# Output weights folded into the key-value sums, queries normalised and turned, one key-query product, and a plain fp32 output projection

## The chip, the cores and the metric

The kernel runs on one core of a Trainium2 chip. Its engines work side by side, each through its own queue of instructions in program order, and wait for one another through semaphores: PE (TensorE, matrix products into PSUM), DVE (VectorE), ACT (ScalarE), POOL (GpSimd) and SP (SyncE, which issues DMA transfers here). The metric is the time of one launch in device microseconds (us), the median of several runs.

## The reference

Input x has 4 batches of 2,048 tokens with 256 features. In fp32:

```
x = x + attn_a(layernorm(x))    # linear attention, 16 heads of 16
x = x + ffn(layernorm(x))       # square(relu(x @ Ws1)) @ Ws2, and routed experts
x = x + attn_b(layernorm(x))    # softmax attention, changes the first 16 tokens of a batch
x = x + ffn(layernorm(x))

# attn_a:
q = elu(x @ Wq + bq) + 1;  k = elu(x @ Wk + bk) + 1;  v = x @ Wv + bv
kv  = einsum('bkhd,bkhm->bhdm', k, v)
out = einsum('bqhd,bhdm->bqhm', q, kv)
normalizer = max(einsum('bqhd,bkhd->bqh', q, k), 1e-6)
out = (out / normalizer[..., None]).reshape(B, S, D) @ Wo + bo
```

The experts' weights are truncated, so they count only if a flag says that some weight reached 1; with these inputs the flag is 0 and the branches on it (`routed > 0`) are not taken.

## The kernel before, in words

The 8,192 tokens are 16 groups (`NG`) of 512, each of 4 tiles (`T`) of 128 tokens; D = 256 is C = 2 blocks of 128. x stays in SBUF (`x_all`) for the whole launch.

**Pass 1** goes over the 16 groups: layer norm 1, transposes of the normalised tokens, the key product by tokens (24 matmuls of 256 columns, operands split into a high and a low part), the query product by features (12 matmuls of 512 columns), exponentials, and G = kᵀx (`g_product`, L1334 and L1339: 8 of 512 and 8 of 256 columns). After each batch the sum G is turned and multiplied with Wv (`kv_product`), masked by head, and stored in `kv_all` with a column per head for the key sums. The queries stay in SBUF, features on partitions (`q_all`).

**Pass 2** goes over steps i = 0 to 17. Step i does the attention output of group i, the first FFN of group r = i − 1 and the second FFN of group v = i − 2. A piece of the small attention attn_b, on the 16 first tokens of each batch, is called in slots between them (`chain(i, slot)`); steps 3 and 4 have no such piece. On PE a step is, in order: T2, transposes of x of group r (L1473); o, queries by key-value sums with the norm in extra columns (L1483); the second FFN's down product (`down`, L1462, into PA); the first FFN's up product (f1, L1504); OT, transposes of the normalised o (L1510); r2, 1/variance turned (L1517); W, the output projection, 24 matmuls of split operands (L1538, L1539, L1544); f3 (L1548); and the first FFN's down product (L1462, into PB).

DVE's queue in a step: the norm out of PSUM (L1035), its reciprocal (L1039), 1/variance (`reciprocal_variances`, L1014, semaphore `rsq`), o times the norm (L1045), the second FFN's sum for two tiles (`scaled_sum`, L1023), o_lo, the low part of the turned o (L1064), h2s (L1071), x plus W (w_add, L1079) with its statistics (bn2, L1003), x plus the FFN (L1087) with its statistics (bn3, L1003). ACT scales the second FFN's other two tiles (`scale_tiles`, L736) into y3. POOL makes the variances (`four_variances`, L491 to L498, five operations for each of the two norms), adds a row to x (`add_row`, L452, 128x1024: `bo` in pass 1, `ob` in pass 2) and adds y3 to x (L550, 128x512). The order of each queue is the order of these calls in the text; no planner moves anything.

Of the kernel before, what the change touches and what calls it, by code (L numbers as in the profile page):

```python
# [13 lines left out]
P = 128  # L14
# [4 lines left out]
T = 4  # L19
# [25 lines left out]
def hybrid_kernel(nc, x_in, Wq, bq, Wk, bk, Wv, bv, Wo, bo, qw, qb, kw, vw, vb, ow, ob,  # L45
# [18 lines left out]
    with ExitStack() as ctx:  # L64
# [11 lines left out]
        q_all = sb("q_all", [P, NG * C, GT])  # L76
        kv_all = sb("kv_all", [P, B * C, KVW])
# [3 lines left out]
        wo_hi, wo_lo = sb("wo_hi", [P, C, D], F32R), sb("wo_lo", [P, C, D], F32R)  # L81
# [17 lines left out]
        norm_sb = sb("norm_sb", [P, T * C, HC])  # L99
        norm_inv = sb("norm_inv", [P, T * C, HC])  # L100
# [31 lines left out]
        o_tok = part(T * D).rearrange("p (k n) -> p k n", k=T * C)  # L132
        x2t = part(C * GT).rearrange("p (c n) -> p c n", c=C)
        h2, h3 = part(GT), part(GT)
        y3 = part(T * D // 2).rearrange("p (t d) -> p t d", d=D)
        token_of = part(B * P)
        squares = o_tok.rearrange("p k n -> p (k n)").rearrange("p (c n) -> p c n", c=C)

        with ExitStack() as pass1_memory:
# [10 lines left out]
            wq_hi, wq_lo = sb1("wq_hi", [P, C, D]), sb1("wq_lo", [P, C, D])  # L150
            wk_hi, wk_lo = sb1("wk_hi", [P, C, D]), sb1("wk_lo", [P, C, D])
            xt_hi, xt_lo = sb1("xt_hi", [P, C, GT]), sb1("xt_lo", [P, C, GT])
            part = parts(sb1("wvo", [P, 9 * D], F32))
            g_sb = part(C * D).rearrange("p (c n) -> p c n", c=C)
            wv = part(C * D).rearrange("p (c n) -> p c n", c=C)
            bo_rows = part(D)
            wo_raw = part(C * D).rearrange("p (c n) -> p c n", c=C)
            wv_last, bv_rows = part(D), part(D)

        part = parts(sb("ffn_weights", [P, 5376 - GT])[:, :])  # L160
        w1c = part(C * F).rearrange("p (c f) -> p c f", c=C)
# [25 lines left out]
        raw4 = [b_weights[:, 1, i, :].rearrange("p (c n) -> p c n", c=C) for i in range(4)]  # L187
        folded_all = b_weights[:, 0, :, :].rearrange("p i n -> p (i n)")
# [18 lines left out]
        used_q = [carve(q_all[:, b * G * C:(b * G + 1) * C, :].rearrange("p k n -> p (k n)")) for b in range(B)]  # L207
# [4 lines left out]
        after_raw = carve(b_weights[:, 1, :, :].rearrange("p i n -> p (i n)"))  # L212
# [8 lines left out]
        later_q = [carve(q_all[:, (b * G + 1) * C:(b * G + 2) * C, :].rearrange("p k n -> p (k n)")) for b in range(B)]  # L221
# [7 lines left out]
        def one_batch_columns(wide):  # L229
# [1484 lines left out]
```

## Time and profile before

| | |
|---|---|
| median of 3 runs | 434.23 us (433.89 to 434.29) |
| span of the profiled execution | 432.7 us |
| PE busy | 416.6 us (96%) |
| DVE busy | 316.3 us (73%) |
| ACT busy | 217.6 us (50%) |
| POOL busy | 217.1 us (50%) |
| granted clock of PE, mean | 0.997 |

The profile has a record of one execution. The span runs from its first to its last instruction; the median of the runs is 1.5 us longer than the span. Busy shares are averages over stages. The views used below are the busy times, windows over stretches of the span, timelines (one line for each instruction or run of like ones, with start and duration), and the instructions of one source line. "L1462" is line 1462 of the kernel before; lines of the changed kernel are told as such.

### The profile page before, as it was taken

The page shows a single profiled execution, that of the slowest core. Times are in us where ns is not written, and L with a number is a line of the kernel's source. Part 1 is how long each engine was busy: PE and PEld are TensorE (multiplying, and loading weights), DVE is VectorE, ACT ScalarE, POOL GpSimd, SP SyncE. Part 2 cuts the span into 40 slices and gives each one's busy share as a digit, 9 for nine tenths or more (in the row PEclk, how much of TensorE's full clock was granted, in tenths as well). Part 3 has the DMA queues.
Part 4 walks back from the last instruction along what each step waited for, and adds up shares of the span by engine and source line. Part 5 has one row for each costly group of instructions (what it writes and reads, how often), then busy time and mean ns, then how long its engine had stood idle before and what let it go on. Part 6 is the DMA issues. An engine that isn't in the chain of part 4 may idle for free.

```text
span 432.7 us, 7753 instructions
## 1 busy us (share of the span) xinstructions
PE 416.6 (96%) x2570; PEld 345.7 (80%) x2570; DVE 316.3 (73%) x707; ACT 217.6 (50%) x383; POOL 217.1 (50%) x317
## 2 busy tenths in 40 slices
PE   8998999999999999899999999999999999999993
PEld 5787889988987988889788886787887787787862
DVE  6769977676668766647878887877778767787864
ACT  3766777778777775326434342343244324334341
POOL 3675776776677764031345336534516416514532
PEclk9999999999999999999999999999999999999998
DMA  8701221111100000300110111011001010011103
GB/s 264 245 7 46 57 88 54 51 49 48 48 0 0 2 2 1 101 0 6 51 52 20 36 51 52 2 51 50 21 31 35 18 52 27 26 51 50 50 4 106
DMA packets 22793, 20.59 MB, mean 48 GB/s; under 512 B 3271, under 2 KB 22733, under 8 KB 22733
## 3 DMA queue, kind: packets, MB, share of 16 engines
q1 hardware_dynamic: 22172, 19.32, 14.1%
q8 instruction: 30, 0.49, 0.5%
q10 hardware_dynamic: 560, 0.52, 0.4%
q14 instruction: 31, 0.25, 0.2%
HBM read 11.32 MB, written 8.45 MB: 46 GB/s over the span
## 4 chain that ended last, share of the span: by engine, by line
PE 68%; DVE 8%; ACT 7%; POOL 7%; issue 5%; SPq 2%; DMA 1%; DVEq 1%; POOLq 0%; ACTq 0%
PE PB L1462 7%; PE PT L1504 6%; PE PA L1462 6%; PE PB L1483 6%; PE PA L1538 4%; PE PA L1544 4%; PE PA L1539 3%; PE PT L1548 3%; PE PA L1473 3%; ACT scratch L568 3%; PE PB L1510 3%; POOL ln_rstd L441 2%; PE PG L1334 2%; POOL ln_rstd L439 2%; DVE ln_bn L800 2%
## 5 line engine op out<-in xcount | busy, mean ns | idle before, releaser
L491 POOL TENSOR_TENSOR ln_a<-ln_bn 128x4 f32<-128x4 f32 x32 | 6.5, 203 | 136.1 <-DVE ln_bn L1003 136.1
L463 POOL TENSOR_TENSOR xn_pair<-scratch,xn_pair 128x1024 fp32r<-128x1024 f32 x16 | 38.4, 2402 | 18.9 <-ACT xn_pair L579 18.9
L883 DVE SCALAR_TENSOR_TENSOR scratch<-scratch,PB 128x512 f32<-128x512 f32 x32 | 20.9, 684 | 36.4 <-ACT scratch L615 36.3
L1003 DVE BATCH_NORM_STATS2 ln_bn<-x_all 128x6 f32<-128x256 f32 x128 | 44.9, 412 | 0.9
L568 ACT ACTIVATE scratch<-x_all,ln_shift,ln_rstd 128x255 f32 (+1 forms) x60 | 31.2, 593 | 22.6 <-POOL ln_shift L445 22.6
L452 POOL TENSOR_TENSOR x_all<-x_all,wvo 128x1024 f32 (+1 forms) x16 | 38.6, 2410 | 0.1
L452 POOL TENSOR_TENSOR x_all<-x_all,ob_rows 128x1024 f32<-128x1024 f32 x16 | 37.7, 2356 | 0.0
L1307 PE MATMUL PB<-wk_hi,xt_hi 128*128 128x256 f32 x128 | 36.9, 288 | 0.6 <-DVE xt_lo L828 0.4
L1309 PE MATMUL PB<-wk_hi,xt_lo 128*128 128x256 f32 x128 | 36.2, 283 | 0.0
L1308 PE MATMUL PB<-wk_lo,xt_hi 128*128 128x256 f32 x128 | 36.2, 283 | 0.0
L736 ACT ACTIVATE scratch<-PA,ln_rsq 128x256 f32<-128x256 f32 x30 | 12.6, 471 | 45.4 <-PE PA L1462 40.2
L1334 PE MATMUL PG<-xn_pair,o_hi 128*128 128x512 f32 x128 | 33.7, 405 | 1.1 <-ACT o_hi L623 1.1
L1079 DVE TENSOR_TENSOR x_all<-PA,x_all 128x1024 f32<-128x1024 f32 x16 | 19.6, 1225 | 19.5 <-PE PA L1544 19.5
L758 ACT ACTIVATE o_hi<-PB 128x512 fp32r<-128x512 f32 x32 | 17.4, 594 | 32.5 <-PE PB L1510 32.5
L1538 PE MATMUL PA<-wo_hi,o_hi 128*128 128x256 f32 x128 | 33.4, 293 | 0.0
L774 ACT ACTIVATE scratch<-PT,w1ob 128x512 f32<-128x512 f32 x16 | 11.0, 688 | 42.1 <-PE PT L1548 42.1
L1539 PE MATMUL PA<-wo_lo,o_hi 128*128 128x256 f32 x128 | 31.9, 282 | 0.0
L1462 PE MATMUL PB<-ws,h2s 128*128 128x256 f32 x128 | 31.0, 385 | 0.0
L1504 PE MATMUL PT<-scratch,ffn_weights 128*128 128x512 f32 x64 | 30.9, 605 | 0.0
L1462 PE MATMUL PA<-ws,scratch 128*128 128x256 f32 x128 | 30.2, 379 | 0.0
L1064 DVE TENSOR_TENSOR o_lo<-PB,o_hi 128x512 fp32r<-128x512 f32 x32 | 20.6, 686 | 12.0 <-ACT o_hi L758 11.8
L1462 PEld LDWEIGHTS PB<-ws,h2s 128*128 128x128 f32 x128 | 23.6, 190 | 6.6 <-issue 3.9
(247 smaller groups left out, 1139.0 us busy)
## 6 DMA issues: line engine op xcount, KB each, us to landing
x_all<-n_L_attn_a_inputs_q_dram SPq DMA_DIRECT2D x15, 512.0 KB, 3.5
out_dram<-x_all SPq DMA_DIRECT2D x15, 512.0 KB, 3.1
out_dram<-x_all SPq DMA_DIRECT2D x2, 256.0 KB, 2.2
x_all<-n_L_attn_a_inputs_q_dram ACTq DMA_DIRECT2D x2, 128.0 KB, 3.0
x_all<-n_L_attn_a_inputs_q_dram SPq DMA_DIRECT2D x2, 128.0 KB, 2.7
setup<-in_L_attn_a_Wk_dram SPq DMA_DIRECT2D x1, 256.0 KB, 4.6
setup<-in_L_attn_a_Wq_dram ACTq DMA_DIRECT2D x1, 256.0 KB, 5.0
wvo<-in_L_attn_a_Wv_dram SPq DMA_DIRECT2D x1, 256.0 KB, 6.7
```

The costliest lines, as they stand in the source:

```text
L452: nc.gpsimd.tensor_tensor(x_group(n), x_group(n), rows_[:, :].rearrange("p (o d) -> p o d", o=1).to_broadcast([P, T, D]), ALU.add).then_in ...
L463: nc.gpsimd.tensor_tensor(xn_pair[:, :, 1, :], xn[g % 2], xn_pair[:, :, 0, :].bitcast(F32), ALU.subtract).then_inc(x_lo, 1)
L568: nc.scalar.activation(dst[:, t:t + 1, 0:width], x_tile(n, t)[:, :, 0:width], ACT.Identity, scale=ln_rstd[:, slot, t:t + 1], bias=ln_shift ...
L1003: nc.vector.bn_stats(ln_bn[:, slot, t:t + 1, :], x_tile(n, t)).then_inc(bn, 1)
L1307: mm(dst, hi, wk_hi[:, c, :], start=(c == 0), stop=False)
L1308: mm(dst, hi, wk_lo[:, c, :], start=False, stop=False)
L1309: last = mm(dst, lo, wk_hi[:, c, :], start=False, stop=(c == C - 1))
L1334: mm(PG[:, c, :], k_hi[:, t, c * P:(c + 1) * P], xn_pair[:, t, :, :].rearrange("p h d -> p (h d)"), start=(g == 0 and t == 0), stop=False, ...
L1462: last = mm(four(pair)[:, t, :], h[:, t * P:(t + 1) * P], ws2[:, :], start=True, stop=True)
L1504: last = mm(PT[:, 0, :], w1c[:, c, :], x2t[:, c, :], start=(c == 0), stop=(c == C - 1))
L1538: mm(four(PA)[:, t, :], hi, wo_hi[:, c, :], start=(c == 0), stop=False)
L1539: mm(four(PA)[:, t, :], hi, wo_lo[:, c, :], start=False, stop=False)
```

## The change

1. **Folded weights.** After each batch, `m_product` multiplies the masked key-value sums with Wo and keeps `m_sum[b]` (256x256); the key sums are kept as one row of 256 for all partitions (`ksum`). In pass 2 the o product is gone.
2. **Queries by token.** Key and query weights stand side by side, so that one product by tokens gives both (24 matmuls of 512 columns; L1322 to L1324 go). `q_all` has tokens on partitions. POOL multiplies queries by key sums (`q_product`), DVE sums by head, bounds, inverts, and multiplies the queries in place (`query`), and PE turns the normalised queries. `query(i + 1)` is called in step i.
3. **Plain fp32 projection.** W is 8 matmuls of fp32 operands; the split of Wo and o_lo are gone.
4. **Smaller moves.** All four tiles of y3 are scaled by ACT and added by POOL (128x1024), save for the last two groups (`by_dve`); the variances of both norms are five POOL operations after bn3 (`variances`); x plus the FFN is added in two halves; the loops over batches in pass 1 are unrolled, its work goes by halves of a group, and `fold_ffn` moves ahead of the last G product.

```diff
+            def q_product(j):  # POOL
+                n, b = lagged(j // B, j % B, 0)[1:]
+                pool.wait_ge(ksum_done, b + 1)
+                pool.wait_ge(q_done, 2 * (n + 1))
...
+                    pool.wait_ge(q_norm, 3 * (j - 1) + 1)
+                nc.gpsimd.tensor_tensor(prod.rearrange("p (t d) -> p t d", t=T), q_all[:, n * T:(n + 1) * T, :],
+                                        ksum[:, b:b + 1, :].to_broadcast([P, T, D]), ALU.mult).then_inc(q_prod, 1)
...
+            def query(j):  # DVE
+                n = lagged(j // B, j % B, 0)[1]
+                by_head = q_all[:, n * T:(n + 1) * T, :].rearrange("p t (h e) -> p (t h) e", e=HD)
+                dve.wait_ge(q_prod, j + 1)
+                nc.vector.reduce_sum(norm_sb[:, :], prod.rearrange("p (k e) -> p k e", e=HD), AX).then_inc(q_norm, 1)
+                dve.wait_ge(q_norm, 3 * j + 1)
+                nc.vector.tensor_scalar(norm_sb[:, :], norm_sb[:, :], NORM_EPS, None, ALU.max).then_inc(q_norm, 1)
+                dve.wait_ge(q_norm, 3 * j + 2)
+                nc.vector.reciprocal(norm_inv[:, :], norm_sb[:, :]).then_inc(q_norm, 1)
+                dve.wait_ge(q_norm, 3 * j + 3)
+                nc.vector.tensor_tensor(by_head, by_head, norm_inv[:, :].unsqueeze(2).to_broadcast([P, T * H, HD]),
+                                        ALU.mult).then_inc(q_ready, 1)
...
+            def m_product(b):  # PE
+                pe.wait_ge(kv_masked, C * (b + 1))
+                pe.wait_ge(ksum_done, b + 1)
+                for c in range(C):
+                    last = mm(PG[:, 1, c * D:(c + 1) * D], kvt[:, c, :], wo_raw[:, c, :], start=True, stop=True)
+                last.then_inc(m_mm, 1)
...
-                    for tiles in ((0, 2), (1, 3)):
+                    pe.wait_ge(m_done, b + 1)
+                    for t in range(T):
                         for c in range(C):
-                            pe.wait_ge(o_hi_done, C * i + c + 1)
-                            for t in tiles:
-                                hi = o_hi[:, c, t * P:(t + 1) * P]
-                                mm(four(PA)[:, t, :], hi, wo_hi[:, c, :], start=(c == 0), stop=False)
-                                mm(four(PA)[:, t, :], hi, wo_lo[:, c, :], start=False, stop=False)
...
+                            pe.wait_ge(ot_copied, C * i + c + 1)
+                            last = mm(four(PA)[:, t, :], o_t[:, c, t * P:(t + 1) * P], m_sum[b][:, c, :],
+                                      start=(c == 0), stop=(c == C - 1))
...
             def scale_tiles(i, v):  # ACT
-                for t in range(2, T):
+                for t in range(by_dve(v), T):
...
             def step(g, b):  # DVE
-                if runs(i):
-                    for c in range(C):
-                        dve.wait_ge(o_hi_done, C * i + c + 1)
-                        nc.vector.tensor_tensor(o_lo[:, c, :], PB[:, c, :], o_hi[:, c, :].bitcast(F32),
-                                                ALU.subtract).then_inc(o_lo_done, 1)
+                if i + 1 < NG:
+                    query(i + 1)
                 if runs(r):
                     dve.wait_ge(f1_sq, r + 1)
```

How the queues move shows best in the instructions themselves. **DVE in step 3 of pass 2.** Before (PT, PA, PB: PSUM; scratch: working rows in SBUF):

```order
L1035 TENSOR_SCALAR norm_sb<-PT 128x16 [waits o_mm]
L1035 TENSOR_SCALAR norm_sb<-PB 128x24 x2
L1039 RECIPROCAL norm_inv<-norm_sb 128x64 [waits o_norm]
L1014 RECIPROCAL ln_rsq<-ln_a 128x8 [waits var3,f4_scaled,r2_mm,var2]
L1045 TENSOR_TENSOR scratch<-PT,norm_inv 128x256 [waits ot_mm,o_norm]
L1045 TENSOR_TENSOR scratch<-PB,norm_inv 128x384 x2
L1023 SCALAR_TENSOR_TENSOR x_all<-PA,ln_rsq,x_all 128x256 [waits c_xs,rsq,f4_mm]
L1023 SCALAR_TENSOR_TENSOR x_all<-PA,ln_rsq,x_all 128x256
L1064 TENSOR_TENSOR o_lo<-PB,o_hi 128x512 [waits w_mm,o_hi_done] x2
L1071 TENSOR_TENSOR h2s<-scratch,PT 128x512 [waits f2_mm,r2_mm,f1_sq]
L1079 TENSOR_TENSOR x_all<-PA,x_all 128x1024 [waits bo_added,w_mm]
```

The changed kernel, from 1/variance (L1056) on:

```order
L1056 RECIPROCAL ln_rsq<-ln_a 128x8 [waits f4_scaled,r2_mm,var]
L943 TENSOR_REDUCE norm_sb<-scratch 128x64 [waits q_prod,rsq,f4_mm]
L945 TENSOR_SCALAR norm_sb<-norm_sb 128x64 [waits q_norm]
L947 RECIPROCAL norm_inv<-norm_sb 128x64 [waits q_norm]
L949 TENSOR_TENSOR q_all<-q_all,norm_inv 128x1024 [waits q_norm]
L1088 TENSOR_TENSOR scratch<-scratch,PT 128x512 [waits r2_mm,f1_sq]
L1096 TENSOR_TENSOR x_all<-PA,x_all 128x1024 [waits bo_added,w_mm]
L1046 BN_STATS ln_bn<-x_all 128x6 [waits var,w_added]
L1046 BN_STATS ln_bn<-x_all 128x6 x3
L1105 TENSOR_TENSOR x_all<-PB,x_all 128x512 [waits f2_mm,ob_added]
L1105 TENSOR_TENSOR x_all<-PB,x_all 128x512 [waits f2_mm]
L1046 BN_STATS ln_bn<-x_all 128x6 [waits var,f2_added]
```

The four instructions of the norm that read PSUM ahead of 1/variance and behind it are gone, with the scaled sum and o_lo. Four instructions of query for the next group, all on SBUF, stand between 1/variance and h2s; w_add and what follows come behind them.

**POOL in the same step.** Before:

```order
L491 TENSOR_TENSOR ln_a<-ln_bn 128x4 [waits bn2,rsq]
L492 TENSOR_TENSOR ln_d<-ln_bn 128x4
L494 TENSOR_SCALAR ln_a<-ln_a 128x4 [waits var2]
L496 TENSOR_TENSOR ln_d<-ln_d 128x4 [waits var2]
L498 TENSOR_TENSOR ln_a<-ln_a,ln_d 128x4 [waits var2]
L491 TENSOR_TENSOR ln_a<-ln_bn 128x4 [waits bn3]
L492 TENSOR_TENSOR ln_d<-ln_bn 128x4
L494 TENSOR_SCALAR ln_a<-ln_a 128x4 [waits var3]
L496 TENSOR_TENSOR ln_d<-ln_d 128x4 [waits var3]
L498 TENSOR_TENSOR ln_a<-ln_a,ln_d 128x4 [waits var3]
L452 TENSOR_TENSOR x_all<-x_all,ob_rows 128x1024 [waits t2_mm]
L550 TENSOR_TENSOR x_all<-x_all,scratch 128x512 [waits f4_scaled]
```

The changed kernel:

```order
L489 TENSOR_TENSOR scratch<-q_all,ksum 128x1024 [waits q_norm,q_done,ksum_done]
L521 TENSOR_TENSOR ln_a<-ln_bn 128x8 [waits bn3,bn2,rsq]
L522 TENSOR_TENSOR ln_d<-ln_bn 128x8
L524 TENSOR_SCALAR ln_a<-ln_a 128x8 [waits var]
L526 TENSOR_TENSOR ln_d<-ln_d 128x8 [waits var]
L528 TENSOR_TENSOR ln_a<-ln_a,ln_d 128x8 [waits var]
L466 TENSOR_TENSOR x_all<-x_all,ob_rows 128x1024 [waits t2_mm]
L582 TENSOR_TENSOR x_all<-x_all,scratch 128x1024 [waits c_xs,f4_scaled]
```

The product q_product stands at the head of the step, the variances of both norms are one run of five, and the sum of y3 covers 1,024 elements where it covered 512.

**DVE at the end of pass 1**, group 15 of the changed kernel (L867: key features, L870: query features, L876: the low part of the keys, for G):

```order
L861 TENSOR_TENSOR xt_lo<-PT,xt_hi 128x2x256 [waits t1_hi]
L867 SCALAR_TENSOR_TENSOR scratch<-scratch,PA 128x512 [waits k_hi_done,kq_exp]
L870 SCALAR_TENSOR_TENSOR q_all<-scratch,PA 128x512
L876 TENSOR_TENSOR o_lo<-scratch,o_hi 128x512 [waits k_hi_done]
L943 TENSOR_REDUCE norm_sb<-scratch 128x64 [waits q_prod]
L945 TENSOR_SCALAR norm_sb<-norm_sb 128x64 [waits q_norm]
L947 RECIPROCAL norm_inv<-norm_sb 128x64 [waits q_norm]
L949 TENSOR_TENSOR q_all<-q_all,norm_inv 128x1024 [waits q_norm]
L867 SCALAR_TENSOR_TENSOR scratch<-scratch,PB 128x512 [waits k_hi_done,kq_exp]
L870 SCALAR_TENSOR_TENSOR q_all<-scratch,PB 128x512
L876 TENSOR_TENSOR o_lo<-scratch,o_hi 128x512 [waits k_hi_done]
```

The query of group 0 stands between the two halves of the last group's features, and waits there for POOL's first q_product.

## Rows read from the trace of the kernel before

**Rows 1.** The page's first part (busy time, share, instructions) and its chain of waits.

```profile
span 432.7 us, 7753 instructions
...
PE 416.6 (96%) x2570; PEld 345.7 (80%) x2570; DVE 316.3 (73%) x707; ACT 217.6 (50%) x383; POOL 217.1 (50%) x317
...
PE 68%; DVE 8%; ACT 7%; POOL 7%; issue 5%; SPq 2%; DMA 1%; DVEq 1%; POOLq 0%; ACTq 0%
```

**Rows 2.** Windows by stage; columns: us, busy of each engine, granted clock, DMA share, GB/s.

```profile
0.00:170.34 170.34, 163.79 (x1006) 141.13 (x1007) 122.31 (x264) 121.45 (x196) 114.99 (x112) 1.00 0.20 61
170.34:197.60 27.26, 25.82 (x197) 23.45 (x196) 16.41 (x38) 9.79 (x21) 3.81 (x7) 1.00 0.16 41
197.60:411.46 213.86, 213.76 (x1312) 171.95 (x1311) 165.71 (x380) 80.22 (x154) 91.90 (x182) 1.00 0.11 37
```

**Rows 3.** Windows: one plain step, one with side chain.

```profile
228.73:242.18 13.45, 13.45 (x83) 11.13 (x82) 10.30 (x24) 5.45 (x10) 5.43 (x12) 1.00 0.13 41
256.09:272.66 16.57, 16.57 (x94) 12.21 (x93) 12.86 (x31) 5.45 (x10) 8.51 (x14) 1.00 0.10 34
```

**Rows 4.** Timeline of the plain step, PE: start, duration, engine, line, operation.

```profile
228.73 1.04 PE L1473 MATMUL PA<-ident,x_all 128*128 128x128 f32 x8
...
229.60 0.63 PE L1483 MATMUL PT<-kv_all,q_all 128*128 128x136 f32 x4
...
231.70 1.89 PE L1462 MATMUL PA<-ws,scratch 128*128 128x256 f32 x8
...
233.43 1.88 PE L1504 MATMUL PT<-scratch,ffn_weights 128*128 128x512 f32 x4
...
236.59 0.36 PE L1538 MATMUL PA<-wo_hi,o_hi 128*128 128x256 f32 x1
...
239.60 1.02 PE L1548 MATMUL PT<-h2s,ffn_weights 128*128 128x512 f32 x2
...
242.18 0.49 PE L1473 MATMUL PA<-ident,x_all 128*128 128x128 f32 x3
```

**Rows 5.** Timeline of the same step, DVE, ACT and POOL.

```profile
230.19 1.41 DVE L1003 BATCH_NORM_STATS2 ln_bn<-x_all 128x6 f32<-128x256 f32 x4
...
232.81 2.35 POOL L452 TENSOR_TENSOR x_all<-x_all,ob_rows 128x1024 f32<-128x1024 f32 x1
233.06 0.20 DVE L1014 RECIPROCAL ln_rsq<-ln_a 128x8 f32<-128x8 f32 x1 [0.21 <-POOL ln_a L498]
...
233.63 0.84 ACT L736 ACTIVATE scratch<-PA,ln_rsq 128x256 f32<-128x256 f32 x2 [3.12 <-PE PA L1462]
...
238.12 0.69 DVE L1071 TENSOR_TENSOR h2s<-scratch,PT 128x512 f32<-128x512 f32 x1 [0.35 <-ACT scratch L766]
...
239.80 1.22 DVE L1079 TENSOR_TENSOR x_all<-PA,x_all 128x1024 f32<-128x1024 f32 x1 [0.99 <-PE PA L1544]
```

**Rows 6.** Timeline, DVE and POOL, at 34 us and at 407 us.

```profile
33.77 2.41 POOL L452 TENSOR_TENSOR x_all<-x_all,wvo 128x1024 f32<-128x1024 f32 x1
...
34.24 2.49 DVE L844 TENSOR_TENSOR wvo<-wvo 128x512 f32<-128x512 f32 x1
...
406.76 1.27 POOL L550 TENSOR_TENSOR x_all<-x_all,scratch 128x512 f32<-128x512 f32 x1
...
406.85 1.32 DVE L1235 TENSOR_SCALAR b_weights<-q_all,ffn_weights 64x256 f32<-64x256 f32 x1
```

**Rows 7.** Instructions of one line: count, duration in ns (least, median, most), first and last start.

```profile
L1039 DVE RECIPROCAL norm_inv<-norm_sb x16: 553/553/554, 175.9 to 403.9; 128x64 f32<-128x64 f32 x16
...
L890 DVE TENSOR_TENSOR o_lo<-scratch,o_hi x16: 1183/1226/2611, 19.8 to 169.9; 128x1024 fp32r<-128x1024 f32 x16
```

**Rows 8.** Timeline, POOL and DVE, at 62.6 us.

```profile
62.54 1.06 POOL L441 TENSOR_TENSOR ln_rstd<-ln_rstd,minus_half 128x4 f32<-128x4 f32 x1
62.62 1.22 DVE L890 TENSOR_TENSOR o_lo<-scratch,o_hi 128x1024 fp32r<-128x1024 f32 x1
```

**Rows 9.** Timeline, PE: the G product of two groups of pass 1.

```profile
143.25 2.11 PE L1334 MATMUL PG<-xn_pair,o_hi 128*128 128x512 f32 x8
...
152.55 2.12 PE L1334 MATMUL PG<-xn_pair,o_hi 128*128 128x512 f32 x8
```

More of the change, by code:

```diff
@@ L318, in runs @@
         def runs(j):
[L320 to L325 removed]
+            return 0 <= j < NG
         @block.sync
@@ L537, in step @@
                 v, nv, _ = lagged(g, b, 2)
[L538 to L542 removed]
+                if i + 1 < NG:
+                    q_product(i + 1)
+                if runs(r) or runs(v):
+                    ge(pool, rsq, i - 1)
+                    variances(i, r, v)
                 if runs(r):
@@ new lines, in _ @@
+            act.wait_ge(consts, 4)
+            x_high(0, 0)
+            normalise(1)
+            for n in range(NG):
+                g, b = n % G, n // G
+                exponentials(n, 0)
+                x_high(n, 1)
+                k_high(n, 0)
+                if n + 1 < NG:
+                    xt_high(n + 1, 0)
+                if g == 0 and b > 0:
+                    transposed_g(b - 1)
+                if n + 2 < NG:
+                    normalise(n + 2)
+                if g == 1 and b > 0:
+                    m_copy(b - 1)
+                exponentials(n, 1)
+                if n + 1 < NG:
+                    xt_high(n + 1, 1)
+                k_high(n, 1)
+                if n + 1 < NG:
+                    x_high(n + 1, 0)
@@ new lines, in _ @@
+            for n in range(NG):
+                g, b = n % G, n // G
+                k_features(n, 0)
+                if g == 0 and b > 0:
+                    copy_g(b - 1)
+                q_features(n, 0)
+                k_low(n, 0)
+                if n + 1 < NG:
+                    xt_low(n + 1, 0)
+                if n + 3 < NG:
+                    stats(n + 3)
+                if n == 1:
+                    dve.wait_ge(w2_loaded, 16 * 8)
+                    take_last_row(wv, wv_last, bv_rows, wv_row, 0.0)
+                if n == NG - 1:
+                    query(0)
+                k_features(n, 1)
+                q_features(n, 1)
+                if g == 0 and b > 0:
+                    batch_kv(b - 1)
+                k_low(n, 1)
+                if n + 1 < NG:
+                    xt_low(n + 1, 1)
@@ new lines, in _ @@
+            for n in range(NG):
+                g, b = n % G, n // G
+                if n == 0:
+                    first_kq()
+                else:
+                    kq(n, 0)
+                    g_product(n - 1, 1)
+                if n + 1 < NG:
+                    t1(n + 1)
+                if g == 0 and b > 0:
+                    g_transposes(b - 1)
+                if g == 1 and b > 0:
+                    m_product(b - 1)
+                if n > 0:
+                    kq(n, 1)
+                if g == 0 and b > 0:
+                    kv_product(b - 1)
+                elif n == 0:
+                    pe.wait_ge(flag_ready, 1)
+                g_product(n, 0)
```

727 lines of the change are left out of this document (322 added, 405 removed).

## The prediction

> **What bounds the kernel now.** I read the page first. TensorE (PE) is busy for 416.6 of 432.7 us and holds 68% of the chain of waits [rows 1]; so far this is a PE-bound kernel. Then the windows by stage: pass 1 takes 170.3 us, the crossing into pass 2 (up to the end of W for group 1) 27.3, the fourteen steps up to the end of W for group 15 take 213.9, and 21.2 remain for the tail. In the fourteen steps PE is busy for 213.76 of 213.86 us at a granted clock of 1.00 (its upper level, 2.4 GHz), VectorE (DVE) for 165.7 and GpSimd (POOL) for 91.9 [rows 2]. A step without side chain takes 13.45 us, all of it PE's, with 10.3 of DVE and 5.4 of POOL; one with a chain takes 16.6, with 12.9 and 8.5 [rows 3]. Matmul records overlap, so I price PE from start to start. Last I read one plain step, first on PE [rows 4], then on the other engines [rows 5].
>
> The span of the profiled execution is 432.7 us, 1.5 below the median of 434.23; I make the sum on the span and add the 1.5 at the end.
>
> **PE's part.** In the plain step the product of queries and key-value sums (L1483) takes 231.70 − 229.60 = 2.10 us. The split W takes 239.60 − 236.59 = 3.01. Both go. The new W is 8 plain fp32 matmuls of 256 columns, two records each. The same form stands at L1462, where 8 records take 233.43 − 231.70 = 1.73, 0.216 each [rows 4]; 16 records take 3.46. Turning the normalised queries replaces turning the outputs, 8 transposes for 8. PE's step becomes 13.45 − 2.10 − 3.01 + 3.46 = 11.8. If PE still bounded, 14 steps and the crossing would give some 25 us back.
>
> **DVE's and POOL's part.** DVE loses the norm and the multiplication from PSUM, the o_lo of the split and the two-tile scaled sum. It gains query(): a reduction of 1,024 elements (I take 1.2, from L1079 at 1.22 for as many elements [rows 5]; half to twice that is possible), a max over 64 (0.2, the size of L1014's 0.20), a reciprocal (0.55, the same form at L1039 [rows 7]) and q times norm_inv over 1,024 (1.2, from L890's 1.23 [rows 7]). By busy time DVE stays near 10.9 us and does not bound. What matters is where it stands: in DVE's queue query() of the next group comes right behind rsq (L1056) and ahead of h2s and w_add, and it meets POOL's two long adds.
>
> What the rows show of that meeting: a DVE addition of 512 elements with both inputs in SBUF lasts 2.49 us while POOL's add_row (L452, 2.41) runs and ends 0.55 after it, although 512 elements need 0.69 at L1071 with one input in PSUM. A TENSOR_SCALAR over 256 lasts 1.32 where POOL's L550 runs, and ends 0.14 after it [rows 6]. DVE instructions that read PSUM are not held: L1079 and the like keep 1.22. A reciprocal keeps 0.553 in all 16 steps [rows 7]. The Trainium skill ("SBUF — State Buffer", section Who interferes with whom) says that DVE's second SBUF input and its two-port modes share a port pair with GpSimd, that whoever issues first holds it for the instruction, and that the other is fully blocked. The trace agrees on the two long additions; it disagrees at POOL's pow, 1.06 us long, beside which L890 with two SBUF inputs keeps 1.22 [rows 8]. By the rule that row would be 0.98 us longer; in pass 2 no pow stands, so my sum is the same either way.
>
> Now a plain step, counted from rsq = R (233.06 in rows 5). add_row runs from R − 0.25 to R + 2.1, as now. The reduction ends at R + 1.4. The max has one input from SBUF, like the held TENSOR_SCALAR: it waits for add_row, ends at R + 2.25, and the reciprocal at R + 2.85. By then POOL is in the sum of y3 (L582, now all four tiles, 2.35 like L452): its last scaled tile comes from ACT at R + 2.15 (L736 begins at R + 0.57; two take 0.84, four 1.58), so it runs to R + 4.5. The multiplication, with two SBUF inputs, waits for that and ends at R + 5.7; h2s, 0.7, at R + 6.4. W could have ended earlier: it needs the scaled tiles out of PSUM (R + 2.15), then 3.46 and 0.2 to DVE [rows 5], R + 5.8. So w_add begins at R + 6.4, held by DVE's queue. Behind it to the next rsq: w_add 1.22, statistics 1.40, f2's addition in two halves 2 × 0.69, statistics 1.40, and POOL's five small operations with their hops 1.46 (statistics end at 231.60, rsq at 233.06). These are 6.9. **The step takes 13.3 us, against 13.45 now**: PE's 1.65 is given to the multiplication's wait, and PE idles 1.5 per step.
>
> Side chains: DVE was busy for 165.71 − 14 × 10.30 = 21.5 us with them in the fourteen steps [rows 2, 3]. Under a full PE that was partly hidden; now DVE's queue is the loop, and it counts in full. In a chained step it stands between rsq and query, or between query and w_add; then the next q_product, which waits only for the reduction, can begin before the multiplication gets its turn, another 2.4 of POOL. From 0 to all of the 12 chained steps can pay it; I take half, 6 × 2.4 = 14.4. Fourteen steps: 14 × 13.3 + 21.5 + 14.4 = 222.1, that is **+8.2** (bounds −6.2 and +22.6).
>
> **Pass 1.** 24 products of 256 columns and 12 of 512 become 24 of 512: the same columns, and the same period of 9.3 [rows 9]. Each batch adds 2 records for ksum and 4 for Wo folded in (m_product), 6 × 0.216 = 1.3 us. If PE waits there anyway for the copies of G, none of it shows; if not, four batches make 5.2. I take 1.5, nearer to nothing, since these records stand between copies. In the first groups the exponentials start only when keys and queries are both there: 1 more. **+2.5** (0 to +6).
>
> **Crossing.** query(0) now stands ahead of the last key features on DVE, and G, the sums of the last batch and everything of pass 2 wait for those. At the least that is query unheld, 1.2 + 0.2 + 0.55 + 1.2 = 3.15, less the 0.55 of today's reciprocal on the same path: +2.6. At the most one addition of bo on POOL holds it for 2.4 more: +5.0. I take the middle, **+3.8**. At nothing I cost the variances in five POOL operations in place of ten (1.46 from statistics to rsq stays, and that is counted above), the gather on SP, which now waits for the turned queries and not for the o product (the chain reads it later), and the unrolled loops of pass 1 (instructions are fetched ahead; if not, pass 1 grows and the range's upper end has it). Tail: 0; the last two groups keep part or all of their sum on DVE.
>
> **Sum**: 432.7 + 8.2 + 2.5 + 3.8 = 447.2, plus the 1.5: **449 us**.
>
> **Rivals.**
> A, faster: the max is not held. Then the reciprocal ends at R + 2.15, before y3's last tile has reached POOL, the multiplication takes the port first and ends at R + 3.35, h2s at R + 4.05; w_add waits for W, R + 5.8, and the step is 12.7. 14 × 12.7 + 21.5 = 199.3, −14.6; with +2.5, +2.6 and the 1.5 that is 424.7, **425 us**. It is decided by whether the reciprocal ends before R + 2.2. For it: the max has 64 elements, the held one 256. Against it: rows 6, and that DVE would have to win in every step. If chains hide under PE too, PE's full 25 us bring 409.
> B, no change: each step is held as I say, but no q_product slips in: 432.7 − 6.2 + 2.5 + 3.8 + 1.5, **434 us**.
> C, slower still: q_product slips in at every chained step, 463, or ahead of the multiplication in plain steps too (+2.4 each), about 468.
> D: PE idles and its clock falls. In the crossing PE is busy for 25.82 of 27.26 at 1.00 [rows 2]; 11.8 of 13.3 is a little less, and nothing speaks for a fall.
>
> **How the numbers follow.** Two measurements of this kernel can be told apart by about 0.2%, 0.9 us. My case, with 3 to 12 slips and the bounds of pass 1 and the crossing, spans 440 to 463 and has 0.62; A 0.20; B, spread over both signs, 0.10; C beyond 464, with D, 0.08. Faster: A and half of B, 0.25. Same: 0.05. Slower: 0.70. The range of 8 in 10 leaves out C and what of A is under 422: 422 to 464.
>
> **What would show it.** Right: PE's busy share in pass 2 falls below 95% while its period grows; L949 lasts well over 1.2 us and ends with POOL's L582 or L489; L945 ends with L466; w_add is released by DVE's own queue, not by W. Wrong: L949 at 1.2 in most steps, or W releasing w_add (A); a plain step of 13.3 and chained ones without a second held multiplication (B); a step under 12 us means that the order on DVE does not bind at all.

## The result, and the profile after

The changed kernel takes **467.97 us** (median of 4 runs, 467.24 to 470.28) against 434.06 beside it on the same chip: a ratio of 1.079, with an interval of 1.076 to 1.083. It is slower, as forecast, but by 34 us where the prediction had 15, and outside the range of 422 to 464. In the experiments below, the kernel before took 432.65 to 434.46 us beside the others, and the changed kernel was not run again, so a difference between kernels of different rounds is known to some 2 us. Two single runs far above the others of their kernel (one of the kernel before, 515.87 us, one of the kernel without the max, 1,439.04) are left out.

The page of the changed kernel, its first part and its chain of waits, beside [rows 1]:

```profile
span 465.5 us, 6522 instructions
...
PE 413.7 (89%) x2170; PEld 329.3 (71%) x2170; DVE 356.0 (76%) x638; ACT 228.8 (49%) x414; POOL 265.2 (57%) x274
...
PEclk9999999999999997998899979899997998889999
...
PE 54%; DVE 26%; issue 12%; POOL 4%; ACT 3%; DVEq 0%; POOLq 0%; ACTq 0%
```

PE does a little less (413.7 us for 416.6) in a longer span, and its share falls from 96% to 89%. The granted clock is no longer full in every slice, and DVE holds 26% of the chain where it held 8%. The windows by stage, cut at the same events as [rows 2] (start of the last group's first G product, end of W for groups 1 and 15), with the tail as a fourth:

```profile
0.00:168.66 168.66, 163.89 (x976) 142.60 (x977) 126.31 (x287) 122.33 (x197) 116.72 (x128) 1.00 0.20 62
168.66:203.00 34.34, 25.69 (x164) 22.58 (x163) 23.57 (x32) 10.89 (x23) 14.86 (x11) 0.90 0.13 32
203.00:445.00 242.00, 210.74 (x975) 154.91 (x974) 194.15 (x292) 89.44 (x182) 128.13 (x124) 0.93 0.09 31
445.00:465.50 20.50, 13.34 (x60) 9.20 (x58) 11.94 (x28) 6.16 (x12) 5.52 (x12) 0.97 0.22 72
```

Pass 1 is 1.7 us shorter than before, the crossing 7.1 longer, the fourteen steps 28.1 longer (242.0 for 213.86), the tail 0.7 shorter. The steps hold the loss. In them DVE went from 165.7 busy us to 194.2 and the clock from 1.00 to 0.93 (part of the time at 1.2 GHz).

A plain step of the changed kernel, timeline of DVE and POOL from rsq (L1056) on; it answers to [rows 5]. L943 to L949 are query, L1096 is w_add:

```profile
229.53 2.36 POOL L466 TENSOR_TENSOR x_all<-x_all,ob_rows 128x1024 f32<-128x1024 f32 x1
...
229.60 0.20 DVE L1056 RECIPROCAL ln_rsq<-ln_a 128x8 f32<-128x8 f32 x1 [1.43 <-POOL ln_a L528]
...
229.90 1.22 DVE L943 TENSOR_REDUCE norm_sb<-scratch 128x64 f32<-128x1024 f32 x1
...
231.15 0.79 DVE L945 TENSOR_SCALAR norm_sb<-norm_sb 128x64 f32<-128x64 f32 x1
...
231.84 2.35 POOL L582 TENSOR_TENSOR x_all<-x_all,scratch 128x1024 f32<-128x1024 f32 x1
231.97 0.55 DVE L947 RECIPROCAL norm_inv<-norm_sb 128x64 f32<-128x64 f32 x1
...
232.56 2.72 DVE L949 TENSOR_TENSOR q_all<-q_all,norm_inv 128x1024 f32<-128x1024 f32 x1
234.16 3.34 POOL L489 TENSOR_TENSOR scratch<-q_all,ksum 128x1024 f32<-128x1024 f32 x1
...
235.20 0.67 DVE L1088 TENSOR_TENSOR scratch<-scratch,PT 128x512 f32<-128x512 f32 x1
235.80 1.21 DVE L1096 TENSOR_TENSOR x_all<-PA,x_all 128x1024 f32<-128x1024 f32 x1
```

The max (L945) ends 0.05 us after add_row, 0.79 us long; the multiplication (L949) ends 1.1 after the sum of y3 (L582), 2.72 long. The step takes 12.90 us from rsq to rsq, 0.55 less than the 13.45 of before. So the plain steps gained, holds and all. A chained step (i = 10), with two of its lines on PE:

```profile
345.83 2.35 POOL L466 TENSOR_TENSOR x_all<-x_all,ob_rows 128x1024 f32<-128x1024 f32 x1
...
346.66 1.81 DVE L1141 TENSOR_TENSOR q_all<-q_all 64x256 f32<-64x256 f32 x1
...
350.07 1.67 DVE L945 TENSOR_SCALAR norm_sb<-norm_sb 128x64 f32<-128x64 f32 x1
...
352.36 3.23 DVE L949 TENSOR_TENSOR q_all<-q_all,norm_inv 128x1024 f32<-128x1024 f32 x1
...
356.24 2.07 PE L1563 MATMUL PT<-scratch,ffn_weights 128*128 128x512 f32 x2 [4.13 <-DVE scratch L1088]
...
358.24 3.68 PE L1651 MATMUL PG<-q_all 128*64 128x128 f32 x16
...
363.13 1.49 DVE L1105 TENSOR_TENSOR x_all<-PB,x_all 128x512 f32<-128x512 f32 x2 [4.17 <-PE PB L1488]
```

L1141, a piece of the chain with two inputs in SBUF that took 0.41 before, takes 1.81 beside add_row; the max takes 1.67, the multiplication, held by y3, 3.23. Then f3 (L1563) takes 2.07 us, where the filled run below has 1.12, and the chain's L1651 3.68; behind both comes the down product, for which DVE waits 4.17 us (L1105). The windows of these two steps:

```profile
229.60:242.50 12.90, 12.29 (x60) 9.37 (x59) 11.21 (x17) 6.18 (x12) 8.90 (x9) 1.00 0.14 45
345.91:368.58 22.67, 18.52 (x81) 13.37 (x80) 16.60 (x25) 6.45 (x13) 12.00 (x11) 0.85 0.07 24
```

### The profile page after: what moved, and what is told of

Read it like the earlier page. It is cut to its first block, busy times and chain, and to the rows that moved or that the text cites. A ratio compares the mean times of both kernels' runs of the same rounds, so it can differ in the third digit from the quotient of the medians.

```text
span 465.5 us, 6522 instructions
## 1 busy us (share of the span) xinstructions
PE 413.7 (89%) x2170; PEld 329.3 (71%) x2170; DVE 356.0 (76%) x638; ACT 228.8 (49%) x414; POOL 265.2 (57%) x274
## 4 chain that ended last, share of the span: by engine, by line
PE 54%; DVE 26%; issue 12%; POOL 4%; ACT 3%; DVEq 0%; POOLq 0%; ACTq 0%
PE PB L1488 5%; DVE ln_bn L1046 5%; PE PA L1558 4%; PE PT L1563 3%; DVE norm_sb L945 3%; DVE norm_sb L943 3%; PE PA L1321 3%; PE PG L1360 3%; PE PB L1323 3%; PE PB L1321 3%; PE PA L1322 3%; PE PB L1322 3%; PE PA L1323 3%; PE PG L1355 3%; PE PG L1356 3%
## 5 line engine op out<-in xcount | busy, mean ns | idle before, releaser
L478 POOL TENSOR_TENSOR xn_pair<-scratch,xn_pair 128x512 fp32r<-128x512 f32 x32 | 41.7, 1304 | 35.5 <-ACT xn_pair L611 35.5
L489 POOL TENSOR_TENSOR scratch<-q_all,ksum 128x1024 f32<-128x1024 f32 x16 | 44.4, 2773 | 15.2 <-DVE norm_sb L943 15.2
L1563 PE MATMUL PT<-scratch,ffn_weights 128*128 128x512 f32 x32 | 22.4, 789 | 28.8 <-DVE scratch L1088 28.8
L949 DVE TENSOR_TENSOR q_all<-q_all,norm_inv 128x1024 f32<-128x1024 f32 x16 | 45.0, 2814 | 0.6
L466 POOL TENSOR_TENSOR x_all<-x_all,wvo 128x1024 f32<-128x1024 f32 x16 | 45.3, 2833 | 0.0
L1558 PE MATMUL PA<-m_early,o_t 128*128 128x256 f32 x192 | 44.2, 383 | 0.0
L1355 PE MATMUL PG<-xn_pair,o_hi 128*128 128x256 f32 x128 | 33.2, 292 | 8.3 <-ACT o_hi L629 8.3
L1558 PEld LDWEIGHTS PA<-m_early,o_t 128*128 128x128 f32 x192 | 35.6, 190 | 5.4 <-issue 0.7
L1488 PE MATMUL PB<-ws,scratch 128*128 128x256 f32 x128 | 36.3, 434 | 0.0
L876 DVE TENSOR_TENSOR o_lo<-scratch,o_hi 128x512 fp32r<-128x512 f32 x32 | 32.1, 1003 | 4.2 <-ACT o_hi L629 2.7
L582 POOL TENSOR_TENSOR x_all<-x_all,scratch 128x1024 f32<-128x1024 f32 (+1 forms) x15 | 34.4, 2291 | 1.3 <-ACT scratch L769 1.3
L1105 DVE TENSOR_TENSOR x_all<-PB,x_all 128x512 f32<-128x512 f32 x32 | 21.3, 684 | 16.6 <-PE PB L1488 16.0
L1356 PE MATMUL PG<-xn_pair,o_hi 128*128 128x256 f32 x128 | 32.2, 285 | 0.0
```

Source lines behind the costliest of these rows:

```text
L466: nc.gpsimd.tensor_tensor(x_group(n), x_group(n), rows_[:, :].rearrange("p (o d) -> p o d", o=1).to_broadcast([P, T, D]), ALU.add).then_in ...
L478: nc.gpsimd.tensor_tensor(halves[:, :, 1, :], pair(xn[n % 2], h), halves[:, :, 0, :].bitcast(F32), ALU.subtract).then_inc(x_lo, 1)
L489: nc.gpsimd.tensor_tensor(prod.rearrange("p (t d) -> p t d", t=T), q_all[:, n * T:(n + 1) * T, :], ksum[:, b:b + 1, :].to_broadcast([P, T, ...
L582: nc.gpsimd.tensor_tensor(last, last, y3[:, by_dve(v):T, :], ALU.add).then_inc(out_pool, 1)
L876: nc.vector.tensor_tensor(pair(k_lo, h), pair(k_tok, h), pair(k_hi, h).bitcast(F32), ALU.subtract).then_inc(k_lo_done, 1)
L949: nc.vector.tensor_tensor(by_head, by_head, norm_inv[:, :].unsqueeze(2).to_broadcast([P, T * H, HD]), ALU.mult).then_inc(q_ready, 1)
```

## The experiments

Theory 1: POOL's long operations hold DVE's instructions that read SBUF, in query and in the side chain, and the rest of the loss follows from that. Theory 2: query costs by its place in DVE's queue, whoever holds what. Theory 3: PE's lower clock is a loss of its own.

**The causes taken apart.** Four kernels from the changed one.

The first cuts the two long additions of POOL in pass 2 to 64 elements:

```diff
-                    add_row(nr, ob_rows, ob_added)
+                    first = x_all[:, nr * T, 0:64]
+                    nc.gpsimd.tensor_tensor(first, first, ob_rows[:, 0:64], ALU.add).then_inc(ob_added, 1)
...
-                    last = x_all[:, nv * T + by_dve(v):(nv + 1) * T, :]
-                    nc.gpsimd.tensor_tensor(last, last, y3[:, by_dve(v):T, :], ALU.add).then_inc(out_pool, 1)
+                    last = x_all[:, nv * T + by_dve(v), 0:64]
+                    nc.gpsimd.tensor_tensor(last, last, y3[:, by_dve(v), 0:64], ALU.add).then_inc(out_pool, 1)
```

> The changed kernel with POOL's two long additions of pass 2 cut from 1,024 elements to 64 each (leaves out most of the row ob and most of the second FFN's sum). Theory 1 (POOL's additions hold DVE's instructions that read SBUF, in the query and in the side chain, and every wait of PE behind them follows from that): L945 falls from 13.3 us in all to some 4 (16 x 0.2, q_product may still meet one or two), L949 from 45 to some 24 (16 x 1.2 and a few meetings with q_product), PE idles less and its clock stays at 1.00; about 425 to 435 us. Theory 2 (the query in DVE's queue delays w_add and the chain by its own length and the chain's hops, whoever holds what): 455 or more. Theory 3 (the time is lost by PE's lower clock, which comes from DVE's new place and not from the holds): the clock stays at 0.93 in pass 2 and the time above 450.

Measured: 437.34 us (435.54 to 437.67), 31 less: 2 us above the range that theory 1 gave, and 18 below that of theory 2. The 16 maxima fell from 16.4 to 7.0 us in all. The multiplication did not: its 16 instances still sum to 44.2 us, where some 24 were expected. It is line 950 in that kernel (count, least, median and most in ns, first and last start); below it, a plain step:

```profile
L950 DVE TENSOR_TENSOR q_all<-q_all,norm_inv x16: 1224/2753/4699, 173.9 to 399.0; 128x1024 f32<-128x1024 f32 x16
```

```profile
226.55 2.36 POOL L489 TENSOR_TENSOR scratch<-q_all,ksum 128x1024 f32<-128x1024 f32 x1
226.71 3.29 DVE L950 TENSOR_TENSOR q_all<-q_all,norm_inv 128x1024 f32<-128x1024 f32 x1
```

With POOL free early, q_product for the next group starts right behind the short additions, 0.16 us ahead of the multiplication, and holds it in the additions' place. So the plain steps stay at 12.88 us, and the gain lies in the chained ones: over the thirteen steps from i = 2 on, the chain's own 57 instructions on DVE fall from 36.3 to 21.8 us in sum of durations, and DVE's idle time by 5.3.

The second puts work on PE, and nowhere else, where it idled:

```diff
                     last.then_inc(w_mm, 1)
+                for _ in range({2: 9, 5: 13, 6: 7, 10: 8, 12: 8, 13: 5}.get(i, 0)):
+                    mm(four(PB)[:, 0, :], o_t[:, 0, 0:P], m_sum[b][:, 0, :], start=True, stop=True)
```

> The changed kernel with matmuls of 256 columns put between W and f3 in the six steps where PE idles for 2.5 us or more there (9, 13, 7, 8, 8 and 5 of them, 0.43 us each, into a PSUM region that is free then, results not used). Nothing on DVE, ACT or POOL changes. Theory 3 as a part of the loss (after such an idle time the granted clock is low, f3 takes 2.07 instead of 1.12 and the down product 3.2 to 3.7 instead of 1.9, and DVE waits for them): these steps keep 1.00 and lose 2 to 3 us each, about 454 us. Theory 1 or 2 alone, with the clock of no weight: 467 to 469, or some more.

Measured: 457.05 us (456.38 to 459.76), 10.9 less with more work. Its windows of step 10 and of the same stretch of time as the third window above (its own fourteen steps lie from 205.08 to 437.80), then its timeline of step 10:

```profile
345.00:365.00 20.00, 19.30 (x97) 14.64 (x96) 16.61 (x24) 6.45 (x13) 12.05 (x12) 1.00 0.09 28
203.00:445.00 242.00, 230.75 (x1114) 173.39 (x1113) 200.43 (x307) 93.93 (x193) 129.66 (x130) 0.99 0.10 33
```

```profile
355.39 1.12 PE L1565 MATMUL PT<-scratch,ffn_weights 128*128 128x512 f32 x2 [0.69 <-DVE scratch L1088]
...
356.44 1.96 PE L1653 MATMUL PG<-q_all 128*64 128x128 f32 x16
...
359.57 1.49 DVE L1105 TENSOR_TENSOR x_all<-PB,x_all 128x512 f32<-128x512 f32 x2 [1.47 <-PE PB L1488]
```

The clock stays at 1.00 in step 10 and f3 is back at 1.12 us, the chain's product at 1.96; the step takes 20.0 us and not 22.67. DVE's holds are as they were (the multiplications sum to 45.7 us). So about 11 of the 34 us are PE's lower clock after it idled. The clock's whole price may be somewhat more: in the profiled run, the slowest of the five, PE idles 2.58 us ahead of f3 in step 7, which was not filled, the granted clock is 0.83 there, and the step takes 20.13 us for 17.47. It is a consequence of DVE's lateness, and has its own price.

The third moves POOL's row addition behind h2s, with all work kept:

```diff
+                chain(i, 1)
                 if runs(r):
                     pool.wait_ge(t2_mm, C * (r + 1))
+                    pool.wait_ge(f1_scaled, r + 1)
                     add_row(nr, ob_rows, ob_added)
-                chain(i, 1)
```

> The changed kernel with POOL's add_row of pass 2 told to wait for h2s (one wait more, and slot 1 of the chain ahead of it), so that add_row, the sum of y3 and q_product run while DVE is at w_add, f2 and statistics, which read PSUM or one input. All work is kept. Theory 1: L945 at 0.2 and L949 at 1.2 in most steps, plain steps at 12.6 to 12.7 (W releases w_add), PE's idle times before f3 under 1 us and its clock at 1.00; 420 to 435 us. Theory 2: no gain from moving the additions, 455 to 470, or worse since the variances of the next step may meet q_product.

Measured: 431.19 us (430.79 to 432.69), ratio to the kernel before 0.996 (0.994 to 0.999). One wait, with slot 1 of the chain moved ahead of it, takes 37 us off the changed kernel and brings it just under the old one; no run has one of the two moves without the other. The max and the multiplication in all 16 groups (least, median, most, in ns), and the timeline of a plain step:

```profile
L946 DVE TENSOR_SCALAR norm_sb<-norm_sb x16: 195/195/1064, 172.3 to 390.9; 128x64 f32<-128x64 f32 x16
...
L950 DVE TENSOR_TENSOR q_all<-q_all,norm_inv x16: 1224/1224/2752, 174.0 to 391.8; 128x1024 f32<-128x1024 f32 x16
```

```profile
224.57 0.20 DVE L1057 RECIPROCAL ln_rsq<-ln_a 128x8 f32<-128x8 f32 x1 [2.06 <-POOL ln_a L528]
...
226.93 1.23 DVE L950 TENSOR_TENSOR q_all<-q_all,norm_inv 128x1024 f32<-128x1024 f32 x1
...
229.20 2.35 POOL L466 TENSOR_TENSOR x_all<-x_all,ob_rows 128x1024 f32<-128x1024 f32 x1 [4.67 <-DVE scratch L1089]
...
230.24 1.22 DVE L1097 TENSOR_TENSOR x_all<-PA,x_all 128x1024 f32<-128x1024 f32 x1 [1.48 <-PE PA L1559]
...
231.51 2.37 POOL L583 TENSOR_TENSOR x_all<-x_all,scratch 128x1024 f32<-128x1024 f32 x1
```

In 14 of 16 groups the multiplication keeps 1.22 (the other two are in the crossing). POOL's long additions (and q_product behind them) now run while DVE is at instructions that read PSUM (w_add, x plus the FFN) or have one input in SBUF (statistics), and none of those is held: w_add keeps 1.22, four statistics 1.41. Theory 2, by which the query's mere place in the queue costs the time, expected 455 or more and falls.

The fourth leaves the max out:

```diff
-                nc.vector.tensor_scalar(norm_sb[:, :], norm_sb[:, :], NORM_EPS, None, ALU.max).then_inc(q_norm, 1)
-                dve.wait_ge(q_norm, 3 * j + 2)
-                nc.vector.reciprocal(norm_inv[:, :], norm_sb[:, :]).then_inc(q_norm, 1)
+                nc.vector.reciprocal(norm_inv[:, :], norm_sb[:, :]).then_inc(q_norm, 2)
```

> The changed kernel without the max of the normalizer (left out; the reciprocal reads the sums as they are). By the step worked out in the prediction the max, held by add_row, is what makes the multiplication miss its turn before the sum of y3. If so (rival A of the prediction): the multiplication, waiting since R + 2.1, takes its turn when add_row ends at R + 2.3 and ends at R + 3.5, POOL's sum of y3 is held until then, and plain steps take 12.7; the chained steps gain more, 455 us or less. If POOL's next addition goes first although DVE has waited longer: L949 is held for some 3.5, plain steps stay at 12.9 and the time at 465 to 468.

Measured: 445.44 us (445.24 to 446.21), 22.5 less. The max takes 0.2 us where nothing holds it, but the 16 maxima of the changed kernel took 16.4. A plain step of it (lines are two lower from the reciprocal on):

```profile
227.67 2.35 POOL L466 TENSOR_TENSOR x_all<-x_all,ob_rows 128x1024 f32<-128x1024 f32 x1
...
229.36 0.55 DVE L945 RECIPROCAL norm_inv<-norm_sb 128x64 f32<-128x64 f32 x1
...
229.95 1.23 DVE L947 TENSOR_TENSOR q_all<-q_all,norm_inv 128x1024 f32<-128x1024 f32 x1
229.99 3.40 POOL L582 TENSOR_TENSOR x_all<-x_all,scratch 128x1024 f32<-128x1024 f32 x1
```

The reciprocal ends before add_row does, the multiplication starts 0.04 us ahead of the sum of y3, keeps 1.23, and now POOL's addition is the one held: 3.40 for 2.35. Plain steps take 12.39 and 12.49, together 0.9 less than in the changed kernel; the rest of the gain lies in the chained steps and isn't taken apart here. This is the point from which rival A was said to decide. By the Trainium skill ("SBUF — State Buffer", section Who interferes with whom), whoever issues first holds the shared ports and the other is blocked for that instruction; the 1.05 us that L582 gained is that, seen from POOL's side.

**The change without the side chain**, and the kernel before without it:

```diff
             def chain(i, slot):
+                if i >= 2:
+                    return
```

> The changed kernel without the small side attention from step 2 on (all pieces of chain left out on all engines; the first 16 tokens of a batch are written as they were gathered). The trace of the changed kernel has two plain steps at 12.90 us, where the one POOL addition holds the max and the next holds the multiplication, and twelve chained ones that take the rest of 242 us. Theory 1 (the loss is what the chain's pieces meet and cause: held themselves, later query, PE idle, lower clock): all steps at 12.9, 468 - (242 - 14 x 12.9) = 407 us, clock 1.00, and no more than the kernel before without its chain (that is 434 - (213.9 - 14 x 13.45) = 409). Rival (the holds of the query alone slow all steps, and the chain is a part of it only): 415 or more, slower than the kernel before without its chain.

> The kernel before without the small side attention from step 2 on, as in the run beside it. All steps at 13.45 us, PE busy throughout: 434 - (213.9 - 14 x 13.45) = 409 us. If the chain hides more than that beside PE: 412 to 420.

Measured: 406.75 us (406.43 to 407.40) and 409.95 (409.67 to 410.12). Every step of the one from i = 2 to 14 takes 12.9 us, of the other 13.45 (the first 13.51). Without the chain the change is a gain of 3 us. The chain costs the kernel before 24 us and the changed one 61. The rival, by which the query's own holds make all steps slower than before, falls.

**One part of the change alone.** The kernel before with W in plain fp32, without the low parts of Wo and o:

```diff
-                    for tiles in ((0, 2), (1, 3)):
...
+                    for t in range(T):
+                        for c in range(C):
+                            pe.wait_ge(o_hi_done, C * i + c + 1)
+                            last = mm(four(PA)[:, t, :], o_hi[:, c, t * P:(t + 1) * P].bitcast(F32), wo_hi[:, c, :].bitcast(F32),
+                                      start=(c == 0), stop=(c == C - 1))
```

> The kernel before with one part of the change alone: W as 8 plain fp32 matmuls on the high parts of Wo and of the turned o (leaves out the low parts; DVE's L1064 is gone). By the prediction's prices PE pays 3.46 for 3.01 in each of 16 steps, and PE is the bound: 434 + 7 = 441 us. If what DVE is freed of (1.29 per step) matters: 434 or less.

Measured: 443.70 us (443.04 to 443.91), 9.3 more than before. Its timeline on PE:

```profile
238.85 3.69 PE L1529 MATMUL PA<-wo_hi,o_hi 128*128 128x256 f32 x16
242.38 1.02 PE L1534 MATMUL PT<-h2s,ffn_weights 128*128 128x512 f32 x2
```

W takes 242.38 − 238.85 = 3.53 us against 3.01 split [rows 4], a plain step 13.97 for 13.45. As long as PE bounds, the split is the cheaper form on PE, and what DVE is freed of buys nothing.

**Toward a version that beats both.** From the kernel with the late row addition, the sum of y3 by halves (two tiles on DVE out of PSUM, as in the kernel before):

```diff
-            return {NG - 2: T // 2, NG - 1: T}.get(v, 0)
+            return T if v == NG - 1 else T // 2
...
                 dve.wait_ge(rsq, i)
+                if v < B:
+                    dve.wait_ge(c_xs, 16 * (v + 1))
                 for t in range(by_dve(v)):
```

> As the run with POOL's add_row behind h2s (431 us), and the second FFN's sum shared as in the kernel before: two tiles on DVE out of PSUM, two by ACT and POOL (512 elements). Theory 1 with POOL's queue as the next bound (in that run the variances wait for q_product in some steps, and W waits for four tiles scaled by ACT): two tiles fewer on ACT let W begin 0.6 us earlier, POOL is free 1.1 earlier, DVE does 0.9 more where it waits for W anyway; plain steps 12.0 to 12.2, about 423 to 426 us. Rival (DVE's queue is the loop, each instruction more on it counts): 14 x 0.86 = 12 more, about 440.

Measured: 430.01 us (429.14 to 432.22), where 423 to 426 was expected. Steps 3 and 4 fell from 12.84 and 12.55 to 12.71 and 12.25 us, less than half of what was hoped. The same kernel once more:

> The version with POOL's add_row behind h2s and the sum of y3 by halves once more, in five rounds, for an interval on the gain over the kernel before. From the earlier runs: 430 us, 0.7 to 1.2% faster.

Measured: 429.92 us (four runs), ratio 0.989 (0.987 to 0.991). This is the best version of the study. A window that holds its fourteen steps:

```profile
203.00:411.00 208.00, 202.56 (x1001) 150.83 (x1000) 163.05 (x327) 81.88 (x161) 111.79 (x126) 1.00 0.11 37
```

PE is busy for 202.6 of these 208.0 us, at full clock. From end of W to end of W (204.97 to 407.90) the fourteen steps take 202.9 us, 11 fewer than the 213.86 of before. But W of group 1 ends 7.2 us later than before (197.76), so pass 1 and the crossing take back more than half of the gain. Then the query of group 0 moved out of the last group's features, and G's transposes ahead of the queries' on PE and ACT, with the rest as in the kernel with the late row addition:

```diff
-                if n == NG - 1:
-                    query(0)
                 k_features(n, 1)
...
                 if i == 0:
+                    query(0)
                     batch_kv(B - 1)
```

> As the run with POOL's add_row behind h2s (431 us), and the query of group 0 moved behind the last features of pass 1 and behind 1/variance of step 0 (PE and ACT turn G ahead of the queries there). It tells what of the crossing's growth comes from the query's place. If all of the idle time of 6.94 us before the last G product is the query's and its holds: 4 to 7 us less, 424 to 427. If DVE is late there anyway (features by halves): 430 to 432.

Measured: 431.27 us, no change. PE's idle time of 6.94 us in the crossing became one of 1.23 and one of 4.49, and the second ends with the multiplication of query(0) itself (L950, 2.74 us long there): what came earlier waited later. Both moves together:

> Both moves together on the changed kernel: POOL's add_row behind h2s, the sum of y3 by halves, and the query of group 0 behind the last features. If the two gains are apart from each other: 416 to 421 us, 3 to 4% faster than the kernel before. If the crossing's gain is taken back in step 0: 423 to 426.

Measured: 430.36 us (429.81 to 431.85), ratio 0.992 (0.989 to 0.995); not better than the halves alone. What else the crossing waits for stays open.

## Why the prediction was right or wrong

**Right: the mechanism, its place and a plain step.** From rsq at 229.60 the prediction had the reduction's end at R + 1.4, the max's at 2.25, the reciprocal's at 2.85, the multiplication's at 5.7, h2s's at 6.4, and a step of 13.3. The rows above have 1.52, 2.34, 2.92, 5.68, 6.27 and 12.90. Of the 0.4 too much, half lies ahead of w_add and half behind it, where queued instructions overlap by some hundredths each. Over fourteen steps that is 5.6 us on the side of slower. That instructions which read PSUM are not held was read from L1079, beside which POOL is idle in [rows 5]; it holds all the same, since L1096 keeps 1.21 us beside q_product in the rows above.

**Right: PE's prices.** The plain W measured 3.53 us (3.46 predicted).

**Right in sum only, by luck: pass 1 and crossing.** +2.5 (0 to +6) and +3.8 (+2.6 to +5.0) were forecast; −1.7 and +7.1 came, +5.4 for 6.3. Both lie outside their bounds, and the errors cancel. In part it is the cut, which lies at the first half of the last group now. The crossing waits for that group's features, behind query(0):

```profile
171.01 1.22 DVE L943 TENSOR_REDUCE norm_sb<-scratch 128x64 f32<-128x1024 f32 x1 [2.28 <-POOL scratch L489]
...
178.06 0.55 PE L1355 MATMUL PG<-xn_pair,o_hi 128*128 128x256 f32 x1 [6.94 <-ACT o_hi L629]
```

Its max and multiplication are held there for 2.3 us in all, and before it DVE waits 2.28 us for POOL's first q_product, which the forecast had at nothing. PE idles 6.94 us before that group's second G product, which then runs at 1.2 GHz (0.21 us from start to start, for 0.12 in pass 1).

**Wrong: the side chain's term.** This is the step that failed. "Now DVE's queue is the loop, and it counts in full" was 21.5 for the chain's pieces at their old durations plus 14.4 for q_products that slip in, and nothing for time in which DVE waits for PE. The thirteen steps from 210.66 to 438.79 take 228.1 us, 60.4 more than 13 × 12.9. Along DVE, with each instruction counted from the end of the one before it, that is made of three terms:

- the chain's own instructions on DVE, 34.5 us, where 21.5 was forecast (in sum of durations the same 57 instructions took 23.2 before and take 36.3 now). Most of the held ones stand right behind rsq, and add_row starts just before rsq. They have two inputs in SBUF (L1175 takes 2.26 for 0.41, L1141 1.81 for 0.41), but a copy with one is held too (L1170, 2.24, where the run with short additions has 0.42).
- held maxima and multiplications beyond a plain step's 3.5 us: 5.4, where 14.4 was forecast. q_product does slip in, but mostly in place of the hold by y3, not on top of it. In one step it came on top, and held the max: in the timeline of step 5

```profile
255.70 2.26 DVE L1175 TENSOR_TENSOR q_all<-q_all,ob_rows 64x256 f32<-64x256 f32 x1
...
259.53 2.34 POOL L582 TENSOR_TENSOR x_all<-x_all,scratch 128x1024 f32<-128x1024 f32 x1
259.76 5.03 DVE L945 TENSOR_SCALAR norm_sb<-norm_sb 128x64 f32<-128x64 f32 x1
261.81 0.62 POOL L546 MEMSET q_all<- 128x640 f32 x1
...
262.41 2.33 POOL L489 TENSOR_TENSOR scratch<-q_all,ksum 128x1024 f32<-128x1024 f32 x1
...
267.29 2.08 PE L1563 MATMUL PT<-scratch,ffn_weights 128*128 128x512 f32 x2 [6.25 <-DVE scratch L1088]
```

the max waits through the sum of y3, a memset and q_product, 5.03 us, and PE then 6.25 for h2s.

- DVE's idle time beyond the 1.7 of a plain step: 20.5, not in the forecast at all. h2s is late, PE waits with f3, and the chain's products and the down product come one after another behind it while DVE waits for them. In the run with the filled gaps this term is 11.4, so 9.1 of it went with the lower clock. That the rest is PE's work, which had been hidden and now is not, is how I read it; no run separates it.

Against the 222.1 us forecast for the fourteen steps, 242.0 came. The plain steps' price was 5.6 too high and the slips' 9.0; the chain's pieces were 13.0 too low and DVE's idle time 20.5 (these terms are of thirteen steps; 1 us is left). So the forecast missed by less than its largest error, since errors of both signs met.

**Wrong: rival D.** "Nothing speaks for a fall" of the clock was read from averages: 11.8 of 13.3 us busy. The idle time is not spread; it is one piece, 4.55 us in step 2, 6.25 in step 5, 4.13 in step 10, each between W and f3, and the granted clock over these steps is 0.82, 0.84 and 0.85. The sum of a late DVE was right in its sign, but its worst steps set PE's clock, and those I had not worked out.

Rival A's rule of decision, the reciprocal's end before y3, was right to within 0.1 us, as the run without the max shows; it had 425 us, and the run in which the maxima and multiplications of the steps aren't held gave 431.

## What to carry to other kernels

An instruction on VectorE whose operands move from PSUM to SBUF can be held by GpSimd. In this kernel that struck instructions with two inputs in SBUF, a max over 64 elements and a copy, and not the reduction; what counted was which long GpSimd operation was due in the same stretch. Order the two queues against each other before counting busy time (here one wait on POOL and one moved slot, worth 37 us). When another engine becomes late in some steps only, work out these steps one by one: here TensorE's idle time came in pieces of 2.5 to 6.3 us in six of the steps, the granted clock fell after them, and work that had been hidden began to count.

## What the runs showed that was not expected

- Which side goes first was decided by 0.04 us: with the max taken out, the multiplication of a plain step came ahead of the sum of y3 and not behind it.
- A held DVE instruction took its turn when one POOL operation ended (L949 ahead of q_product in plain steps), but not in step 5, where a memset stood between two additions; there the max waited for three operations.
- The reduction over 1,024 elements in SBUF was never held: 1.15 to 1.22 us in all 16 groups, beside add_row or not.
- Beside POOL's pow of 64x16 (L555, 2.91 us) the max took 1.67 us in two steps, where a pow in [rows 8] had left a subtraction with two inputs in SBUF (L890) at 1.22. Whether it was the pow that held it isn't settled: the max ended 0.4 us before it.
